# A graph attention and feed-forward kernel: rounded passes on three source tiles instead of one, two of their low parts made by DMA, and earlier loads

## The chip, the cores and the metric

One core of one Trainium2 chip runs the whole program. The metric is the device time in microseconds (us) of one execution, the median of several runs; lower is better.

## The reference

There are N = 1250 nodes with 768 features and 21,250 edges (a list of random pairs in both directions, and one loop per node). Two graph attention layers are followed by a feed-forward block.

```
def gat_layer(x, W, att_src, att_dst, bias, src, dst, heads, out_ch):
    h = (x @ W.T).reshape(n, heads, out_ch)
    e = leaky_relu(a_src[src] + a_dst[dst], 0.2)
    m = segment_max(e, dst);  ex = exp(e - m[dst])
    alpha = ex / (segment_sum(ex, dst)[dst] + 1e-16)
    return segment_sum(alpha[:, :, None] * h[src], dst) + bias

h   = relu(gat_layer(layernorm(x), W1, ..., heads=8, out_ch=128))
x   = x + gat_layer(h, W2, ..., heads=1, out_ch=768)
out = x + ffn(layernorm(x))     # six class tokens take a routed path
```

The change lies almost wholly in the first layer, with its eight heads.

## The kernel before

Attention is dense. A 1250 by 1250 matrix holds the logarithm of the number of edges between each destination and each source (LC, ten tiles of 125 destinations). For a head, the logits of 125 destinations against all 1250 sources are one tile L of 125 by 1250, and L is turned by TensorE so that sources lie on the partitions and the sum over sources is a matmul.

The first layer's loop runs over steps. A step n is one head h = n / 5 (rounded down) and one pair g of destination tiles; there are 5 steps a head and 40 in all. A pair of heads shares one pass of the loop, so k runs from 0 to 9. For step n:

- VectorE makes two logit tiles (L2061, one instruction each), then subtracts the log counts and takes the largest (L2070, one each). It also takes the reciprocals of the sums (L2038, L2040) for 10, 6 or 4 tiles at a time, three times for two heads, and once a head copies one column set (L2052).
- ScalarE takes the exponentials of the two tiles (L897, an ACTIVATE and a read of its accumulator each) and counts `exp_done` up once, after the second.
- TensorE waits for `exp_done` and turns the two tiles with 20 transposes of 125 by 125 into five PSUM banks (L1385), four to a bank, in groups of two source tiles by 250 destinations. After each bank it counts `tb_full`.
- ScalarE copies each bank into the tile PT in SBUF (L915 and, for one bank, L912 and L913), which counts `tb_evac`.
- TensorE sums over the ten source tiles into 125 by 250 of PSUM (L1409), features h1s times PT. A float32 matmul is shown as two instructions. One source tile, number PART = 2, goes in three passes with operands rounded to a shorter format (float32r): high times high, low times high, high times low (L1414 to L1416). ScalarE makes the high parts (L912, L924) and VectorE the low ones by subtraction (L2082, L2087).
- ScalarE copies the sums to hT (L948).

The first head (steps 0 to 4) takes all ten source tiles in float32.

What runs in what order on an engine is fixed by the program. TensorE in its step k does the turning of step k-1, then the sums of step k-2. ScalarE in its step k does this:

```
evac(hh, k)          # the banks of step k-1
exp(hh, k)           # the exponentials of step k
part_higher(hh, k)   # once a head
rows_out_of(hh, k)   # three times for two heads (L936)
sums_out(hh, k)      # the sums of step k-3
```

VectorE in its step k does the logits of step k and then the low part of step k-1. SyncE issues the loads of a head's logits (asb, 1250 KB, a broadcast to all partitions, L488), its features (L483) and small stores of reciprocals; GpSimd does nothing in this stage. Ahead of step k = 6 of the first pair of heads TensorE needs W2 (w2n_sb, 3 MB, L455) for 48 small instructions (L1446). After the last head come the product with W2 (L1481), the second layer and the feed-forward block, which the change leaves alone but for names of semaphores.

## Time and profile before

| | |
|---|---|
| median of 3 runs | 715.89 us (714.38 to 720.05) |
| the profiled execution | 714.73 us |
| its span, first to last instruction | 712.9 us |
| granted TensorE clock, mean | 0.999 of full speed, in the records of every slice 0.9 or more |
| TensorE busy | 700.6 us, 98% |
| VectorE, ScalarE, GpSimd busy | 529.0, 420.3, 106.3 us |

Of the execution's time 1.8 us lie outside the span. Times below are of that one execution, counted from the start of its span. "Busy" is the time in which at least one instruction of the engine is in flight, so a busy engine isn't always one at its peak: a matmul is shown longer than the distance to the next one. What counts for rate is the distance between starts.

### The profile page before, as it was taken

To read this page: it belongs to the slowest core of one execution; us is meant where nothing else is said; L and a number is where in the kernel's file an instruction comes from. 1 tells how busy PE (TensorE), PEld (TensorE's weight loads), DVE (VectorE), ACT (ScalarE), POOL (GpSimd) and SP (SyncE) were. 2 spreads that over 40 slices of the span, in tenths; PEclk is the share of its full clock that TensorE was granted. 3 is DMA by queue.
4 is the path that set the end of the run, shared out by engine and by line. 5 is a ranking of instruction groups with operands and counts; after the bars stand their busy time and mean duration, and the time that the engine had idled before them with its cause. 6 is when DMAs were issued, how large, how long until landed. Compare 5 with 4: busy or idle time off the path is not lost.

```text
span 712.9 us, 13401 instructions
## 1 busy us (share of the span) xinstructions
PE 700.6 (98%) x4670; PEld 657.0 (92%) x4670; DVE 529.0 (74%) x878; ACT 420.3 (59%) x863; POOL 106.3 (15%) x95
## 2 busy tenths in 40 slices
PE   7899999999999999999999999999999999999997
PEld 6699999889799999999999999999999899999997
DVE  5999888698899999999999664445568752737232
ACT  4665584388688889888888754454443333522202
POOL 2558121000000000000000000000123331222202
PEclk9999999999999999999999999999999999999999
DMA  8727656649321212302330443201881735315102
GB/s 284 221 64 202 198 181 174 175 137 315 116 73 37 73 37 73 108 21 88 87 126 0 105 110 71 61 0 36 247 281 55 215 91 189 100 58 176 44 23 67
DMA packets 50226, 84.10 MB, mean 118 GB/s; under 512 B 14633, under 2 KB 35951, under 8 KB 49280
## 3 DMA queue, kind: packets, MB, share of 16 engines
q1 hardware_dynamic: 44492, 65.69, 30.6%
q10 hardware_dynamic: 4500, 13.82, 5.9%
q0 software_dynamic: 1184, 3.92, 1.9%
q8 instruction: 31, 0.51, 0.3%
q14 instruction: 19, 0.16, 0.1%
HBM read 68.09 MB, written 15.33 MB: 117 GB/s over the span
## 4 chain that ended last, share of the span: by engine, by line
PE 87%; DMA 6%; DVE 3%; SPq 1%; ACT 1%; issue 1%; POOL 0%; ACTq 0%; DVEq 0%
PE bank L1409 19%; PE bank L1554 13%; PE bank L1481 12%; PE bank L1281 11%; PE bank L1385 11%; PE bank L1658 4%; PE bank L1630 3%; DMA w1n_sb<-in_W 3%; PE bank L1196 3%; DMA w2n_sb<-in_W 2%; PE bank L1535 2%; PE bank L1684 1%; DVE x2f L2295 1%; PE bank L1198 1%; PE bank L1211 1%; PE bank L1715 1%
## 5 line engine op out<-in xcount | busy, mean ns | idle before, releaser
L1409 PE MATMUL bank<-PT,h1s 125*128 125x250 f32 x730 | 161.0, 374 | 0.0
L1409 PEld LDWEIGHTS bank<-PT,h1s 125*128 125x128 f32 x730 | 135.3, 190 | 14.4
L2061 DVE SCALAR_TENSOR_TENSOR L<-asb,nadh 125x1250 f32<-125x1250 f32 x80 | 117.9, 1514 | 1.9 <-PE bank L1385 0.9
L2070 DVE CUSTOM_DVE_ANT_0 L<-L,LC 125x1250 f32<-125x1250 f32 x80 | 113.4, 1454 | 0.6 <-DMA LC<-log_count_scratch 0.4
L897 ACT ACTIVATE L<-L,nm 125x1250 f32<-125x1250 f32 x80 | 108.3, 1383 | 2.7 <-DVE nm L2070 1.9
L915 ACT COPY PT<-bank 125x500 f32<-125x500 f32 x165 | 87.4, 611 | 36.5 <-PE bank L1385 36.5
L1385 PE MATMUL bank<-ident,L 125*125 125x125 f32 x800 | 94.2, 273 | 0.0
L1385 PEld LDWEIGHTS bank<-ident,L 125*125 125x125 f32 x800 | 91.2, 189 | 0.9 <-issue 0.4
L1867 DVE TENSOR_TENSOR hotr<-iota,r 125x1500 f16<-125x1500 f16 x50 | 46.5, 931 | 8.1 <-PE bank L1198 4.5
L1554 PE MATMUL bank<-h_hi,PT_hi 125*125 125x384 f32 x200 | 41.5, 350 | 0.0
L1554 PE MATMUL bank<-h_lo,PT_hi 125*125 125x384 f32 x200 | 40.4, 342 | 0.0
L726 POOL MEMSET pick<- 128x90 f32 x1 | 0.2, 169 | 268.0 <-ACT hT L948 268.0
L1037 ACT ACTIVATE L<-L,nm 125x1250 f32<-125x1250 f32 x10 | 13.4, 1341 | 42.3 <-DVE nm L2215 42.3
L1554 PE MATMUL bank<-h_hi,PT_lo 125*125 125x384 f32 x200 | 38.1, 336 | 0.0
L1554 PEld LDWEIGHTS bank<-h_hi,PT_hi 125*125 125x125 f32 x200 | 34.0, 185 | 2.5 <-ACT PT_hi L1045 0.7
L2147 DVE COPY as2c<-bank 125x1 f32<-125x1 f32 x10 | 1.6, 158 | 45.6 <-ACT h_hi L1000 45.6
L1554 PEld LDWEIGHTS bank<-h_hi,PT_lo 125*125 125x125 f32 x200 | 35.1, 185 | 0.0
L1554 PEld LDWEIGHTS bank<-h_lo,PT_hi 125*125 125x125 f32 x200 | 34.9, 186 | 0.0
L702 POOL TENSOR_TENSOR x<-x,b_sb 125x768 f32<-125x768 f32 x10 | 19.0, 1901 | 103.6 <-DMA fc2b_sb<-in_fc2b 93.4
L987 ACT ACTIVATE hT<-hT,b_sb x64 | 19.5, 387 | 24.6 <-DVE hT L2122 24.6
L2272 DVE TENSOR_TENSOR x2f<-bank,x2f 125x384 f32<-125x384 f32 x20 | 10.2, 551 | 29.5 <-PE bank L1658 27.9
L1630 PE MATMUL bank<-yT,fc_sb 128*128 128x250 f32 x144 | 31.3, 375 | 0.0
(285 smaller groups left out, 1345.1 us busy)
## 6 DMA issues: line engine op xcount, KB each, us to landing
asb<-src_logit_rows SPq DMA_DIRECT2D x7, 1250.0 KB, 5.8
atom_w<-in_atom_inT SPq DMA_DIRECT2D x5, 1152.0 KB, 12.7
atom_w<-in_atom_outT SPq DMA_DIRECT2D x5, 1152.0 KB, 9.8
log_count_scratch<-LCw SPq DMA_DIRECT2D x10, 546.9 KB
LC<-log_count_scratch SPq DMA_DIRECT2D x10, 546.9 KB
LCt<-log_count_scratch SPq DMA_DIRECT2D x10, 546.9 KB
h_scratch<-h1st ACTq DMA_DIRECT2D x10, 448.0 KB
rdT<-reciprocal_scratch SPq DMA_DIRECT2D x8, 500.0 KB, 4.6
```

What stands on the lines that cost most here:

```text
L897: e = act.activation(L[r][:, :], L[r][:, :], ACT.Exp, bias=nm[q][:, t:t + 1], scale=-1.0, accum_out=den[q][:, t:t + 1])
L915: act.copy(PT[(k - lag) % 2][:, 2 * b:2 * b + 2, :], turned[0:NP, 0:2 * GW].rearrange("p (s n) -> p s n", s=2)).then_inc(tb_evac, 1)
L1281: mm = pe.matmul(bank[b][0:NP, 0:c1 - c0], rows[t % 2][:, k, :], weights[:, k, c0:c1], start=(part == 0 and k == 0), stop=(part == 2 and k ...
L1385: mm = pe.transpose(bank[turned_bank(first, k - lag, b)][0:NP, (2 * s + j) * NP:(2 * s + j + 1) * NP], L[(2 * (k - lag) + j) % 4][:, (2 * ...
L1409: mm = pe.matmul(sums, h1s[q][:, s, :], PT[p][:, s, :], start=(s == 0), stop=(plain and s == NT - 1))
L1481: mm = pe.matmul(bank[2 * p + b][0:NP, 0:w], rows[p][:, k, :], weights[:, k, c0:c0 + w], start=(part == 0 and k == 0), stop=(part == 2 and ...
L1554: mm = pe.matmul(bank[2 + 2 * j + b][0:NP, 0:HALF], rows[:, s, j * NP:(j + 1) * NP], features[:, s, b * HALF:(b + 1) * HALF], start=(term ...
L1630: mm = pe.matmul(bank[6 + m // 2][:, (m % 2) * GW:(m % 2 + 1) * GW], fc1_sb[:, k, m * 128:(m + 1) * 128], yT[:, k, :, :].rearrange("p j n ...
L1658: mm = pe.matmul(bank[down_bank(i, j) + b][0:NP, 0:HALF], rows[:, m, j * NP:(j + 1) * NP], weights[:, m, b * HALF:(b + 1) * HALF], start=( ...
L1867: dve.tensor_tensor(hotr[w][:, :, :, :], iota2[:, 0:GW, :].unsqueeze(1).to_broadcast([CE, TRIP, GW, 2]), r16[:, ds(2 * pair, 2 * TRIP)].re ...
L2061: dve.scalar_tensor_tensor(L[r][:, :], asb[q][0:NP, 1, :], nadh[q][:, t:t + 1], asb[q][0:NP, 0, :], ALU.add, ALU.max).then_inc(stt_done, 1)
L2070: dve.tensor_tensor_reduce(out=L[r][:, :], in0=L[r][:, :], in1=LC[:, t, :], scale=-1.0, scalar=-FLOOR, op0=ALU.add, op1=ALU.min, accum_out ...
```

## The change

Source tiles 0, 1 and 2 of the first layer's sums go in rounded passes instead of tile 2 alone (heads 1 to 7; the first head stays as it was). Tile 0's low part is made by VectorE, as that of tile 2 was. The low parts of tiles 1 and 2 are made by GpSimd's DMA queue: ScalarE writes the turned tile once as it is and once rounded, one of the two with its sign turned, one transfer copies the first into PT_sum, and a second one adds the other to it. The head's first logit loads are split in four, W2 turned (w2n_sb) is loaded during the stage before, W2 itself (w2_sb) in eight pieces during the loop. Some buffers share memory that had their own.

```diff
-PART = 2
+QUARTERS = 4
+PART = 0
...
+                if i == 1:
+                    sp.wait_ge(wattp, 1)
+                else:
+                    load_w2n(i - 2)
...
-            sp.wait_ge(wattp, 1)
-            for k in range(KD):
-                load_w2n(k)
...
                     sp.wait_ge(stt_done, NT * (2 * hh + q) + NT)
-                    load_logits(q, 2 * hh + q + 2)
+                    load_logits(q, 2 * hh + q + 2, 0)
                     (store_even, store_odd_last)[q](hh)
+                    for b in range(1, 3):
+                        sp.wait_ge(stt_done, NT * (2 * hh + q) + (NT + 2 * b))
+                        load_logits(q, 2 * hh + q + 2, b)
                     sp.wait_ge(agg_done, NG * (2 * hh + q) + NG)
                     load_features(q, 2 * hh + q + 2)
-            sp.wait_ge(wattp, 3)
-            sp.dma_start(w2_sb[:, :, 0:D], W2T.rearrange("(k p) n -> p k n", p=128)).then_inc(w2_in, 16)
+                    sp.wait_ge(stt_done, NT * (2 * hh + q) + (NT + 6))
+                    load_logits(q, 2 * hh + q + 2, 3)
+                    sp.wait_ge(wattp, 3)
+                    sp.wait_ge(stt_done, NT * (2 * hh + q) + (NT + 8))
+                    load_w2(2 * hh + q)
...
+            def lower_by_sum(hh, kk):
+                n, p = 2 * NG * hh + kk, kk % 2
+                pool.wait_ge(tb_evac, NG * n + 2)
+                alone(pool)
+                pool.dma_start(PT_sum[p][:, :, :].bitcast(F32), PT[p][:, 1:3, :]).then_inc(raw_moved, 16)
+                pool.wait_ge(raw_moved, 16 * n + (16 - 16 * NG))
+                alone(pool)
+                pool.dma_start(PT_sum[p][:, :, :].bitcast(F32), PT_hi[p][:, 1:3, :].bitcast(F32), accum_op=ALU.add
+                               ).then_inc(lower_moved[p], 16)
...
                     if b == PART // 2 and not (first and k - lag < NG):
-                        act.copy(PT_hi[(k - lag) % 2][:, :], turned[0:NP, 0:GW])
-                        act.copy(PT[(k - lag) % 2][:, PART + 1, :], turned[0:NP, GW:2 * GW]).then_inc(tb_evac, 1)
+                        act.copy(PT_hi[(k - lag) % 2][:, 0:2, :],
+                                 turned[0:NP, 0:2 * GW].rearrange("p (s n) -> p s n", s=2))
+                        act.activation(PT[(k - lag) % 2][:, 1, :], turned[0:NP, GW:2 * GW], ACT.Copy, scale=-1.0
+                                       ).then_inc(tb_evac, 1)
+                    elif b == 1 and not (first and k - lag < NG):
+                        act.copy(PT[(k - lag) % 2][:, 2:4, :],
+                                 turned[0:NP, 0:2 * GW].rearrange("p (s n) -> p s n", s=2))
+                        act.activation(PT_hi[(k - lag) % 2][:, 2, :], turned[0:NP, 0:GW], ACT.Copy, scale=-1.0
+                                       ).then_inc(tb_evac, 1)
...
-                act.copy(h1p[q][:, 0, :], h1s[q][:, PART, :]).then_inc(features_high, 1)
+                act.activation(h1p_neg[q][:, :, :], h1s[q][:, 1:3, :], ACT.Copy, scale=-1.0)
+                act.copy(h1p_hi[q][:, :, :], h1s[q][:, 0:3, :]).then_inc(features_high, 1)
...
-                    pe.matmul(sums, h1p[q][:, 0, :], PT_hi[p][:, :], start=False, stop=False)
-                    pe.matmul(sums, h1p[q][:, 1, :], PT_hi[p][:, :], start=False, stop=False)
-                    mm = pe.matmul(sums, h1p[q][:, 0, :], PT_lo[p][:, :], start=False, stop=True)
+                    for s in range(3):
+                        high = h1p_neg[q][:, 1, :] if s == 2 else h1p_hi[q][:, s, :]
+                        pe.matmul(sums, high, PT_hi[p][:, s, :], start=False, stop=False)
+                        pe.matmul(sums, h1p_lo[q][:, s, :], PT_hi[p][:, s, :], start=False, stop=False)
+                    pe.matmul(sums, h1p_hi[q][:, 0, :], PT_lo[p][:, :], start=False, stop=False)
+                    pe.wait_ge(lower_moved[p], 16 * NG * hh + 16 * ((k - lag) // 2 - (NG // 2 - p)))
+                    pe.matmul(sums, h1p_neg[q][:, 0, :], PT_sum[p][:, 0, :], start=False, stop=False)
+                    mm = pe.matmul(sums, h1p_hi[q][:, 2, :], PT_sum[p][:, 1, :], start=False, stop=True)
...
-                    dve.tensor_tensor(h1p[q][:, 1, :], h1s[q][:, PART, :], h1p[q][:, 0, :].bitcast(F32), ALU.subtract
-                                      ).then_inc(features_lower, 1)
+                    dve.tensor_tensor(h1p_lo[q][:, 0:2, :], h1s[q][:, 0:2, :], h1p_hi[q][:, 0:2, :].bitcast(F32),
+                                      ALU.subtract)
+                    dve.tensor_tensor(h1p_lo[q][:, 2, :], h1p_hi[q][:, 2, :].bitcast(F32), h1s[q][:, 2, :],
+                                      ALU.subtract).then_inc(features_lower, 1)
```

## Rows read from the trace of the kernel before

**Rows 1.** Busy time, the sum over four heads, 209.43 to 336.87 us.

```profile
sum 127.44, PE 127.44 PEld 119.48 DVE 123.90 ACT 110.33 POOL 0.00; mean PE 31.86 PEld 29.87 DVE 30.97 ACT 27.58 POOL 0.00
```

**Rows 2.** Waits from 209 to 395 us: total us, times, longest.

```profile
ACT PT L915 <- PE bank L1385: 25.7, 30, 1.0
DVE dn L2038 <- ACT L L897: 3.0, 6, 0.5
```

**Rows 3.** Timeline of TensorE's weight loads, one step: start, length, instruction.

```profile
311.12 2.27 PEld L1385 LDWEIGHTS bank<-ident,L 125*125 125x125 f32 x20
313.32 3.68 PEld L1409 LDWEIGHTS bank<-PT,h1s 125*128 125x128 f32 x18
317.02 0.19 PEld L1414 LDWEIGHTS bank<-PT_hi,h1p 125*128 125x128 f32 x1
...
317.35 0.19 PEld L1416 LDWEIGHTS bank<-PT_lo,h1p 125*128 125x128 f32 x1
317.47 0.63 PEld L1385 LDWEIGHTS bank<-ident,L 125*125 125x125 f32 x5
```

**Rows 4.** Timeline of ScalarE, the same step.

```profile
311.88 0.58 ACT L915 COPY PT<-bank 125x500 f32<-125x500 f32 x1 [0.71 <-PE bank L1385]
312.35 0.37 ACT L912 CAST PT_hi<-bank 125x250 fp32r<-125x250 f32 x1
312.61 0.39 ACT L913 COPY PT<-bank 125x250 f32<-125x250 f32 x1
312.87 1.57 ACT L915 COPY PT<-bank 125x500 f32<-125x500 f32 x3
314.27 1.39 ACT L897 ACTIVATE L<-L,nm 125x1250 f32<-125x1250 f32 x1
...
315.60 1.38 ACT L897 ACTIVATE L<-L,nm 125x1250 f32<-125x1250 f32 x1
316.83 0.24 ACT L897 ACTIVATION_READ_ACCUMULATOR L<-L,nm 125x1 f32 x1
...
318.22 0.58 ACT L915 COPY PT<-bank 125x500 f32<-125x500 f32 x1 [0.90 <-PE bank L1385]
```

**Rows 5.** Timeline of ScalarE, ahead of that step, where a head begins.

```profile
310.47 0.33 ACT L924 CAST h1p<-h1s 125x128 fp32r<-125x128 f32 x1
310.66 0.25 ACT L936 COPY rrow<-bank 10x125 f32 x1
310.81 0.35 ACT L948 COPY hT<-bank 128x250 f32 x1
```

**Rows 6.** Timeline of VectorE in the same step.

```profile
312.07 0.08 DVE L2070 DVE_READ_ACCUMULATOR2_ANT nm<- 125x1 f32 x1
...
313.45 0.29 DVE L2082 TENSOR_TENSOR h1p<-h1s,h1p 125x128 fp32r<-125x128 f32 x1
313.66 0.41 DVE L2087 TENSOR_TENSOR PT_lo<-bank,PT_hi 125x250 fp32r<-125x250 f32 x1
313.99 2.94 DVE L2061 SCALAR_TENSOR_TENSOR L<-asb,nadh 125x1250 f32<-125x1250 f32 x2
```

**Rows 7.** DMA queues and issues; an issue's size and median us to landing.

```profile
q0 software_dynamic: 1184, 3.92, 1.9%
...
x<-in_x POOLq DMA_DIRECT2D x10, 336.0 KB, 3.6
```

**Rows 8.** Line 698, GpSimd's loads of x: ns of issue, first and last.

```profile
L698 POOL DMA_DIRECT2D x<-in_x x20: 518/552/627, 414.9 to 668.8; - x20
...
DMA to landing us min/median/max: 3.1/3.7/8.7
```

**Rows 9.** Waits of TensorE, 130 to 215 us.

```profile
PE bank L1446 <- DMA w2n_sb<-in_W: 0.8, 1, 0.8
```

**Rows 10.** Timeline behind the last turning, 400 to 404 us.

```profile
402.21 0.42 DVE L2087 TENSOR_TENSOR PT_lo<-bank,PT_hi 125x250 fp32r<-125x250 f32 x1 [5.50 <-ACT PT L913]
...
402.97 0.27 PE L1430 MATMUL bank<-ident,rden 125*4 125x125 f32 x1 [0.20 <-DVE rden L2040]
```

More of the change, by code:

```diff
@@ L293, in gnn_ffn_kernel @@
         L = [sb(f"L{r}", [NP, N], F32, p3) for r in range(4)]
+        once = ExitStack()
+        rdA = [sb(f"rdA{p}", [C, H, NP], F32, once) for p in range(2)]
+        once.close()
         asb[1] = sb("asb1", [128, 2, N], F32, p3)
@@ L427, in gnn_ffn_kernel @@
         w1_hi_done, w1_lo_done, xT_lo_done = sem("w1_hi_done"), sem("w1_lo_done"), sem("xT_lo_done")
+        raw_moved, lower_moved = sem("raw_moved"), [sem(f"lower_moved{p}") for p in range(2)]
         features_high, features_lower, lower_done = sem("features_high"), sem("features_lower"), sem("lower_done")
@@ L548, in load_reciprocals @@
                     sp.wait_ge(scaled, t - 1)
+                if t < 2:
+                    sp.wait_ge(stt_done, NT * H)
                 to = (rdA if t < 2 else rdT)[t % 2]
@@ L721, in after_x2 @@
                     add_bias(n + 1)
+            def lower_by_sum(hh, kk):
[7 more added lines that the diff above has]
+                               ).then_inc(lower_moved[p], 16)
+            for kk in range(NG, 2 * NG):
+                lower_by_sum(0, kk)
+            with pool.Fori(1, H // 2) as hh:
+                for kk in range(2 * NG):
+                    lower_by_sum(hh, kk)
             pool.wait_ge(agg_done, NG * H)
@@ L932, in rows_out_of @@
                 act.wait_ge(rden_turned, m + 1)
-                to = rlast[:, ds(hh if k else hh + -1, 1), 0:NP] if (t0, t1) == (LATE, NT) else None
-                if to is None:
-                    to = rrow[t0:t1, ds(h, 1), 0:NP]
-                act.copy(to.rearrange("t a n -> t (a n)"), bank[4][0:t1 - t0, 0:NP]).then_inc(rden_rows, 1)
+                freed(act, rden_stored, 16 * m)
+                act.copy(rrow[0:t1 - t0, 0:NP], bank[4][0:t1 - t0, 0:NP]).then_inc(rden_rows, 1)
             def sums_out(hh, k, first=False, last=False):
@@ L1407, in aggregate @@
                         pe.wait_ge(head_in[q], TWO * (hh + 1))
-                    if plain or s != PART:
-                        mm = pe.matmul(sums, h1s[q][:, s, :], PT[p][:, s, :], start=(s == 0), stop=(plain and s == NT - 1))
+                    if plain or s > 2:
+                        mm = pe.matmul(sums, h1s[q][:, s, :], PT[p][:, s, :], start=(s == (0 if plain else 3)), stop=(plain and s == NT - 1))
                 if not plain:
@@ L1552, in add_5 @@
                     if j == 0 and b == 0 and s % 2 == 0 and term != "hl":
-                        pe.wait_ge(t5_high if term == "hh" else t5_evac, 5 * i + s // 2 + 1)
+                        if term == "hh":
+                            pe.wait_ge(tb_evac, TURNED_BANKS + 5 * i + s // 2 + 1)
+                        else:
+                            pe.wait_ge(t5_evac, 5 * i + s // 2 + 1)
                     mm = pe.matmul(bank[2 + 2 * j + b][0:NP, 0:HALF], rows[:, s, j * NP:(j + 1) * NP],
```

68 lines of the change are left out of this document (41 added, 27 removed).

## The prediction, as it went on record before the run

> **What bounds the kernel now.** I read three things in this order: the busy times of the stage that the change touches, the waits in it, and then the timelines of one step side by side, to see which loop closes last.
>
> TensorE has no gap at all over four heads: 31.86 us a head, all of it busy, while VectorE is busy for 30.97 and ScalarE for 27.58 [rows 1]. In the same stretch ScalarE waits for TensorE 30 times, 25.7 us in all, and VectorE six times for ScalarE, 3.0 us; no wait of TensorE is among them [rows 2]. So TensorE sets the pace, 6.37 us a step.
>
> One step of TensorE is 2.20 us for 20 transposes (311.12 to 313.32), 3.70 for 18 float32 instructions and 0.45 for the three rounded ones, with the switch to them (317.02 to 317.47): 6.35 [rows 3]. A float32 instruction is 3.70 / 18 = 0.21 us, a source tile 0.42. A rounded pass is 0.12 at most (317.35 to 317.47); I use 0.115, and a tile in three passes is about 0.345.
>
> The reader should see how near the others are. ScalarE is not slow by its sum, but it stands in a loop with TensorE: the turning of step n-1 gives the copies of its banks, then come the two exponentials of step n, and only then may TensorE turn step n, since it waits for `exp_done`. In numbers: the turning's first weight load at 311.12 [rows 3], first copy at 311.88, so 0.76; copies until the first exponential at 314.27, 2.39; the two exponentials until the accumulator is read at 316.83 + 0.24 = 317.07, 2.80 [rows 4]. That is 5.95, and the next turning starts at 317.47 [rows 3]: TensorE comes 0.40 us after ScalarE is ready. The loop would close by itself in 5.95 plus the reaction to one semaphore, which no row shows by itself, since nobody waits there now. I bound it by 0 and 0.10, the distance between two transposes (2.20 / 20 = 0.11), and take 0.03, an estimate. 5.98 against 6.35: the slack is 0.37 us a step.
>
> **The change part by part.**
>
> TensorE. Two tiles go from 0.42 to 0.345, so a step loses 4 x 0.21 - 6 x 0.115 = 0.15 us and needs 6.20. Alone over 35 steps that is 5.3 us.
>
> ScalarE, each step. Before, the five banks are four copies of 500 columns and two of 250. After, they are five of 500 and two of 250: bank 0 is rounded whole and its second half written again with the sign turned, bank 1 is copied whole and its first half rounded again. One copy of 500 more: 0.47 us (311.88 to 312.35; three others take 1.40) [rows 4]. A copy with a scale has no row of that shape; it is the same instruction reading the same bank, so I take the 0.26 of the 250-column pieces (312.35, 312.61, 312.87), and its bounds are 0.26 and 0.47, the 500-column pace. All of it stands between the turning and the exponentials, none in ScalarE's idle time, because that idle time lies behind the exponentials. The loop becomes 5.98 + 0.47 = 6.45 us, longer than TensorE's 6.20 and longer than today's 6.35. This is the core of my forecast: 0.15 is taken off the engine that bounds, 0.47 is put into a loop with a slack of 0.37.
>
> ScalarE, once a head. `part_higher` casts 128 columns in 0.19 (310.47 to 310.66), then 0.15 for the reciprocals' row, then the sums [rows 5]. The change makes 256 and 384 columns of it. By the exponential's pace (1250 columns in 316.83 - 315.60 = 1.23, 0.95 us a thousand [rows 4]) they are 0.31 and 0.43. From the second exponential's start ScalarE's next work may begin after about 1.32, and the next bank is ready after 1.47 + 0.03 + 0.76 = 2.26: 0.94 is free. Needed are 0.31 + 0.43 + 0.15 + 0.26 = 1.15, so 0.21 a head comes on top. Bounds: 0 and 0.74.
>
> A head is then 5 x 6.45 + 0.21 = 32.46 against 31.86: +0.60, and seven heads +4.2 us. The steps' scatter by the unknown reaction (0 to 0.10) is -1.0 to +2.4.
>
> VectorE. Per head the subtraction for the features grows from one of 128 columns (0.21, 313.45 to 313.66) to 256 and 128; 250 columns take 0.33 (313.66 to 313.99) [rows 6], so +0.33. With the 30.97 busy of [rows 1] that is 31.3 and with small gaps 31.5 at most, under 32.46: hidden. If ScalarE's loop were not there, this would be the next bound. PT_lo now reads bank 0 and TensorE's next turning of bank 0 waits for it, but it is made right after the largest of the step ahead is taken, at 313.66, and that step's exponentials end 3.4 us later [rows 4, 6]: hidden, and dear only if VectorE falls 3 us behind. Its largest values are ready at 312.15 and 313.53 for exponentials that start at 314.27 and 315.60 [rows 4, 6], so ScalarE doesn't wait for them, and after the change it asks later still.
>
> GpSimd's two transfers. They run each step one behind the other: 125 rows of 2000 bytes, 250 KB, out of SBUF and into it. The nearest row is the load of x: 336 KB land 3.6 us after issue. The queue moved 3.92 MB in 1.9% of 16 engines' span, 217 us of engine time, so 18 KB a microsecond and engine [rows 7]; 336 KB on 16 engines are 1.16 us and the rest, 2.4 us, is fixed. A 250 KB copy is 2.4 + 0.86 = 3.3. No row shows a transfer that adds. It is at least a copy (3.3), and with its destination read as well its data part at most doubles (4.1). I take 4.1, so with 0.2 for two reactions T = 7.6; in 7.0 to 7.6 without other traffic. One load of x took 8.7 [rows 8], 5 more than its median, beside large loads; that is my upper end for traffic.
> Its deadline: if step n is turned at S, bank 1 is copied at S + 0.76 + 2 x (0.47 + 0.26) = S + 2.2. TensorE turns n+1 from S + 6.45 on for 2.2, then does 14 float32 instructions (2.95) and seven rounded ones (0.8), and asks at S + 12.4. So T may be 10.2, and 7.6 is hidden. GpSimd itself is held for the first transfer and two issues of 0.55 [rows 8], some 4.6 of 6.45 us, and has nothing else queued until the last head's sums are out. The last step is turned with no exponentials behind it, and its transfers have only some 7.9 us; T just fits: 0, at most 1.
>
> The Trainium skill (DMA: Bandwidth & Descriptors, Anatomy of one DMA) fits a GpSimd transfer as 2.0 us plus the bytes at 436 KB a microsecond. By it the pair would take an estimated 5.1 us and the deadline would be met with more room; the forecast is the same by either, and the rows' larger value is used above.
>
> Loads. W2 is 0.8 us late for TensorE now [rows 9]; loaded a stage earlier it isn't: -0.8. The six loads stand in SyncE's queue behind the wait for the first stage's small product and between stores and loads of log counts; TensorE has no wait on a DMA from 130 us on but this one [rows 9], so I take 0 for the added traffic, bounds 0 and +2. The queue's logits in four pieces and eight W2 pieces add some ten issues a head and waits on VectorE's logits; each is for a tile that is due a head later. Cost 0; if a store of reciprocals behind them came late, ScalarE would wait for its row buffer, which has become single, but it has three steps or more. W2 itself was there early before: 0.
>
> End of the stage. The last two sums have no exponentials to wait for, so TensorE's 0.15 counts there: -0.3. VectorE's last PT_lo waits for bank 0 instead of bank 1 and with it the 0.20 that TensorE waits for the last reciprocals [rows 10] goes: -0.2.
>
> Sum: +4.2 - 0.8 - 0.3 - 0.2 = +2.9. On the profiled execution's 714.7 that is 717.6 us. Its time lies 1.2 under the median of the three runs, within their spread of 5.7.
>
> **The rivals.**
>
> A. The loop through ScalarE doesn't close as I say (its instructions overlap more, or the scaled copies are cheaper), and TensorE or VectorE bounds. For it: the page's sum leaves ScalarE idle 4.3 us a head [rows 1]. Against it: that idle time lies wholly in front of the first copy of a step, where it waits for TensorE [rows 2, 4]. Price: with TensorE alone -5.3 - 1.0 = 708.4; with VectorE at 31.5 a head -0.36 x 7 - 1.0, 711.2.
>
> B, the slow side. The two transfers miss the deadline in every step. The mechanism: 125 rows don't divide by 16. If a transfer is spread over the largest number of engines up to 16 that divides its rows, that is 5, the data part of a copy is 250 / 5 / 18 = 2.8 and that of an adding one up to 5.6. The pair takes 5.2 + 8.0 + 0.2 = 13.4. It decides from T = 10.2 on: then the loop runs over two steps through PT's two buffers, T + 0.25 + 0.76 + 1.46 long, and a step is (T + 2.5) / 2 = 7.9 us, +1.6 x 35 = 770. If only the adding one is spread so, T = 11.5, a step is 7.0, +22, 738. For it: every long transfer of this program that goes to 125 rows is cut into 112 and 13 (ROWS in the code), the new ones aren't, and no row shows one uncut. Against it: the median over all twenty loads of x, half of them of 13 rows, is 3.7 [rows 8], and that of the large ones 3.6 [rows 7], so the fixed part is most of such a transfer.
> The Trainium skill (DMA: Bandwidth & Descriptors, Why a DMA increments its semaphore by 16 and not by 1) states this rule of the largest divisor, and an exception in which GpSimd's plain copies take all 16 engines with rows rounded up. No row here tells which holds for an adding transfer.
>
> C. T is short enough alone, but not beside the head's features (625 KB in short pieces) or a quarter of the logits: then one or two steps a head run over. By the 8.7 of [rows 8] T is up to 12.6, 2.4 over: seven times 1.2 to 2.4, 726 to 735.
>
> **How the numbers follow.** My forecast has 0.55, A 0.15 (a third of it at TensorE's bound), B 0.18, C 0.12. The likeliest case alone runs from 714 to 721. A measurement of this kernel can tell about 1% from no change, 7 us. The range leaves out the lower end of A and the upper part of B: 709 to 738. Faster by over 1% (under 708.7) is the end of A alone, 0.06. Slower by over 1% (over 723) is B, C and the tail of mine where several upper bounds meet: 0.18 + 0.12 + 0.03 = 0.33. Within 1%: 0.61.
>
> **What would show it.** In the changed kernel's profile a plain step should be 6.45 us between turnings, TensorE should have a gap ahead of most turnings (0.25 us, released by the exponential of L897), ScalarE's wait for bank 0 should shrink to what the first four transposes take, and be gone at a head's beginning. GpSimd's second transfers should land before the last two matmuls ask; a gap inside the sums, released by a DMA to PT_sum, is B or C. The 0.8 us before L1446 should be gone. The forecast is wrong if turnings follow each other in 6.2 to 6.3 us without a gap (A), or if gaps stand inside the sums (B, C).

## The result, and the profile after it

The changed kernel takes 737.38 us (median of 4 runs, 734.57 to 739.14) against 715.68 (714.38 to 720.05) for the kernel before: ratio 1.0307, 95% interval 1.0281 to 1.0334. It is slower by 21.7 us where the forecast was +2.9; 737.4 lies 0.6 us inside the upper end of the range of 709 to 738, an end that stands for another case than the one that came. The profiled execution took 737.6 us, its span is 735.8 us against 712.9, so 22.9 us are to be found. Its mean granted TensorE clock is 0.994, that of before 0.999.

The page of the changed kernel, first the busy times, then its GpSimd DMA queue and the two transfers (KB each, median us from issue to landing):

```profile
PE 708.1 (96%) x4740; PEld 661.9 (90%) x4740; DVE 532.1 (72%) x885; ACT 440.7 (60%) x905; POOL 162.1 (22%) x165
...
q0 software_dynamic: 8464, 21.43, 14.8%
...
PT_sum<-PT POOLq DMA_DIRECT2D x35, 244.1 KB, 3.6
PT_sum<-PT_hi POOLq DMA_DIRECT2D x35, 244.1 KB, 4.2
```

TensorE's share has fallen from 98% to 96%, though its matmuls of a step were to take 0.15 us less. The waits of TensorE over the whole span (us in total, times, longest) say where that is:

```profile
PE bank L1471 <- DMA PT_sum<-PT_hi: 13.1, 8, 3.0
PE bank L1436 <- ACT L L942: 2.8, 15, 0.3
```

L1471 is the first of the two matmuls that read PT_sum: TensorE stands inside the sums, released by the adding transfer. L1436 is the turning, released by the exponentials. Both are waits that [rows 2] does not have. For nearly the same stretch as [rows 2], here 209 to 410 us, the same view has also the waits of the other engines:

```profile
POOL PT_sum L759 <- DMA PT_sum<-PT: 113.9, 29, 6.1
...
ACT PT_hi L957 <- PE bank L1436: 23.5, 23, 2.9
```

Before, ScalarE waited 30 times for bank 0, once for each turning. Now it is 23 times for 29 turnings, up to 2.9 us where TensorE itself came late, and the six turnings without a wait are the ones behind ScalarE's extra work of a head's beginning, as the prediction said.

**An undisturbed step.** The weight loads of TensorE, same view as [rows 3]: a turning begins every 6.62 us, not every 6.35 as in those rows (317.47 less 311.12), and ahead of each there is a gap. For a weight load the view calls what ends the gap "issue"; for the matmul behind it, it names the exponentials of L942, as above:

```profile
244.77 2.26 PEld L1436 LDWEIGHTS bank<-ident,L 125*125 125x125 f32 x20 [0.36 <-issue]
...
251.38 2.26 PEld L1436 LDWEIGHTS bank<-ident,L 125*125 125x125 f32 x20 [0.25 <-issue]
...
308.82 2.26 PEld L1436 LDWEIGHTS bank<-ident,L 125*125 125x125 f32 x20 [0.35 <-issue]
...
315.43 2.26 PEld L1436 LDWEIGHTS bank<-ident,L 125*125 125x125 f32 x20 [0.37 <-issue]
```

ScalarE in the step whose turning begins at 308.82, same view as [rows 4]:

```profile
309.56 0.58 ACT L957 CAST PT_hi<-bank 125x500 fp32r<-125x500 f32 x1 [0.69 <-PE bank L1436]
310.03 0.38 ACT L959 ACTIVATE PT<-bank 125x250 f32<-125x250 f32 x1
310.30 0.58 ACT L962 COPY PT<-bank 125x500 f32<-125x500 f32 x1
310.75 0.41 ACT L964 ACTIVATE PT_hi<-bank 125x250 fp32r<-125x250 f32 x1
311.02 1.57 ACT L967 COPY PT<-bank 125x500 f32<-125x500 f32 x3
312.42 1.40 ACT L942 ACTIVATE L<-L,nm 125x1250 f32<-125x1250 f32 x1
...
313.75 1.38 ACT L942 ACTIVATE L<-L,nm 125x1250 f32<-125x1250 f32 x1
314.98 0.25 ACT L942 ACTIVATION_READ_ACCUMULATOR L<-L,nm 125x1 f32 x1
```

Turning to first copy 0.74 (308.82 to 309.56), copies 2.86 (to 312.42), exponentials 2.81 (to 314.98 + 0.25 = 315.23). The next turning begins at 315.43: 0.20 us after ScalarE is done. This is the loop of the prediction, closed, and the copies with a scale cost what was said, 0.27 for 250 columns (310.03 to 310.30 and 310.75 to 311.02).

**A disturbed step.** GpSimd's timeline has an undisturbed pair of transfers and one beside loads. The idle time in brackets ahead of L759 runs from the end of the first issue to the landing of the copy:

```profile
219.97 0.55 POOL L756 DMA_DIRECT2D PT_sum<-PT  x1 [2.29 <-ACT PT L967]
226.57 0.84 POOL L759 DMA_DIRECT2D PT_sum<-PT_hi  x1 [6.06 <-DMA PT_sum<-PT]
...
247.69 0.55 POOL L756 DMA_DIRECT2D PT_sum<-PT  x1 [2.45 <-ACT PT L967]
251.02 0.84 POOL L759 DMA_DIRECT2D PT_sum<-PT_hi  x1 [2.77 <-DMA PT_sum<-PT]
```

Alone, the copy took 3.3 us from the start of its issue to the start of the next (247.69 to 251.02), that is 2.8 behind the end of its issue of 0.55; the one at 219.97 took 6.6 and 6.1. The median to landing that the views give (3.6) counts from the end of the issue, as its lowest of 2.8 and highest of 6.9 show. SyncE's queue and the windows (us from, to, length; busy of each engine; granted clock; DMA share; GB/s) show what was in the air with it:

```profile
218.34 1.49 SPq L503 DMA_DIRECT2D asb<-src_logit_rows  x2
223.68 0.95 SPq L497 DMA_DIRECT2D h1s<-h_scratch  x2
224.89 0.35 SPq L503 DMA_DIRECT2D asb<-src_logit_rows  x1
```

```profile
219.00:221.00 2.00, 2.00 (x13) 1.85 (x12) 2.00 (x6) 2.00 (x6) 0.55 (x1) 1.00 0.95 170
...
247.00:251.00 4.00, 4.00 (x25) 3.68 (x25) 4.00 (x6) 4.00 (x8) 0.55 (x1) 1.00 0.42 95
...
264.00:266.00 2.00, 0.32 (x3) 0.12 (x1) 1.41 (x3) 0.76 (x3) 0.00 (x0) 1.00 1.05 271
...
267.00:268.00 1.00, 1.00 (x6) 1.00 (x6) 0.80 (x2) 0.34 (x1) 0.43 (x1) 0.50 0.01 3
...
270.00:271.00 1.00, 1.00 (x9) 0.94 (x9) 0.40 (x1) 0.84 (x2) 0.48 (x1) 1.00 0.95 140
```

The copy started on full engines (share 0.95, two quarters of the logits), and the adding transfer then ran into the features and a third quarter. The pair took 11.3 us (219.97 to 231.26) where 7.6 were forecast and 10.2 were to be free. The waits of TensorE that follow, in its timeline:

```profile
231.26 0.39 PE L1471 MATMUL bank<-PT_sum,h1p_neg 125*128 125x250 f32 x1 [1.38 <-DMA PT_sum<-PT_hi]
266.20 0.38 PE L1471 MATMUL bank<-PT_sum,h1p_neg 125*128 125x250 f32 x1 [1.88 <-DMA PT_sum<-PT_hi]
...
425.40 0.38 PE L1471 MATMUL bank<-PT_sum,h1p_neg 125*128 125x250 f32 x1 [1.87 <-DMA PT_sum<-PT_hi]
...
432.62 0.38 PE L1471 MATMUL bank<-PT_sum,h1p_neg 125*128 125x250 f32 x1 [2.95 <-DMA PT_sum<-PT_hi]
432.96 4.52 PE L1537 MATMUL bank<-w_hi,h1Tt_hi 128*125 128x384 f32 x16
```

About one step a head has such a wait, 34 to 36 us apart (203.47, 231.26, 266.20, 301.93, 336.04, 370.56; between the first two it is 28), of 1.1 to 1.9 us, and the last two steps of the stage have 1.87 and 2.95. These eight are the 13.1 us.

**The clock.** Behind the wait of 1.88 us (264 to 266 us, TensorE busy for 0.32 of 2.00), the windows show a granted clock of 0.50, that is 1.2 instead of 2.4 GHz, with TensorE busy all the time; at 270 it is 1.00 again. Its weight loads show what that costs:

```profile
266.47 3.90 PEld L1436 LDWEIGHTS bank<-ident,L 125*125 125x125 f32 x20
...
274.39 2.27 PEld L1436 LDWEIGHTS bank<-ident,L 125*125 125x125 f32 x20
```

The turning takes 3.90 us instead of 2.26 and the step 7.92 instead of 6.62: 1.3 us. Behind the wait of 2.95 the first 16 matmuls of the product with W2 take 4.36 to the next group (432.96 to 437.32); without transfers (the first experiment) it is 3.37, another 1.0 us. But a wait doesn't always bring this. Behind 1.38 the next step is 6.62 long, and behind 1.87, nearly as long as the wait of 1.88, the granted clock stays at 1.00 (425 to 432 us) and the 14 float32 matmuls take 2.77 us as elsewhere.

### The profile page after: what moved, and what is told of

It reads as the page before. It is cut to its first block, busy times and chain, and to the rows that moved or that the text cites. A ratio compares the mean times of both kernels' runs of the same rounds, so it can differ in the third digit from the quotient of the medians.

```text
span 735.8 us, 13937 instructions
## 1 busy us (share of the span) xinstructions
PE 708.1 (96%) x4740; PEld 661.9 (90%) x4740; DVE 532.1 (72%) x885; ACT 440.7 (60%) x905; POOL 162.1 (22%) x165
## 4 chain that ended last, share of the span: by engine, by line
PE 72%; DMA 15%; ACT 6%; DVE 3%; issue 3%; ACTq 0%; POOL 0%; SPq 0%; POOLq 0%; DVEq 0%
PE bank L1613 13%; PE bank L1537 12%; PE bank L1332 11%; PE bank L1460 8%; PE bank L1436 7%; DMA PT_sum<-PT 6%; DMA PT_sum<-PT_hi 5%; PE bank L1717 4%; DMA w1n_sb<-in_W 3%; PE bank L1689 3%; PE bank L1247 3%; ACT L L942 2%; PE bank L1591 1%; PE bank L1743 1%; DVE x2f L2356 1%
## 5 line engine op out<-in xcount | busy, mean ns | idle before, releaser
L1460 PE MATMUL bank<-PT,h1s 125*128 125x250 f32 x590 | 131.4, 374 | 0.0
L1460 PEld LDWEIGHTS bank<-PT,h1s 125*128 125x128 f32 x590 | 108.9, 190 | 11.2
L942 ACT ACTIVATE L<-L,nm 125x1250 f32<-125x1250 f32 x80 | 108.6, 1389 | 2.8 <-DVE nm L2129 1.9
L1436 PE MATMUL bank<-ident,L 125*125 125x125 f32 x800 | 98.2, 279 | 3.8 <-ACT L L942 2.8
L1436 PEld LDWEIGHTS bank<-ident,L 125*125 125x125 f32 x800 | 92.4, 191 | 9.5 <-issue 8.6
L967 ACT COPY PT<-bank 125x500 f32<-125x500 f32 x130 | 67.3, 626 | 2.1 <-PE bank L1436 2.1
L759 POOL DMA_DIRECT2D PT_sum<-PT_hi x35 | 29.6, 845 | 142.8 <-DMA PT_sum<-PT 136.7
L756 POOL DMA_DIRECT2D PT_sum<-PT x35 | 20.9, 596 | 91.0 <-ACT PT L967 91.0
L957 ACT CAST PT_hi<-bank 125x500 fp32r<-125x500 f32 x35 | 20.1, 574 | 31.4 <-PE bank L1436 31.4
```

Source lines behind the costliest of these rows:

```text
L759: pool.dma_start(PT_sum[p][:, :, :].bitcast(F32), PT_hi[p][:, 1:3, :].bitcast(F32), accum_op=ALU.add).then_inc(lower_moved[p], 16)
L942: e = act.activation(L[r][:, :], L[r][:, :], ACT.Exp, bias=nm[q][:, t:t + 1], scale=-1.0, accum_out=den[q][:, t:t + 1])
L967: act.copy(PT[(k - lag) % 2][:, 2 * b:2 * b + 2, :], turned[0:NP, 0:2 * GW].rearrange("p (s n) -> p s n", s=2)).then_inc(tb_evac, 1)
L1436: mm = pe.transpose(bank[turned_bank(first, k - lag, b)][0:NP, (2 * s + j) * NP:(2 * s + j + 1) * NP], L[(2 * (k - lag) + j) % 4][:, (2 * ...
L1460: mm = pe.matmul(sums, h1s[q][:, s, :], PT[p][:, s, :], start=(s == (0 if plain else 3)), stop=(plain and s == NT - 1))
```

## The experiments

Each was timed against the kernel before on the same chip, whose medians were 714.5 to 715.3 us in these comparisons. Theory: two costs that add, the loop through ScalarE (copies with a scale, nothing else) and transfers that miss their deadline only beside loads. Rivals: the transfers are too slow by themselves (the prediction's B), or the time is lost elsewhere, in the early loads or in GpSimd's use of the queue.

**1. No transfers.** ScalarE does all its work, TensorE all its passes.

```diff
-            for kk in range(NG, 2 * NG):
-                lower_by_sum(0, kk)
-            with pool.Fori(1, H // 2) as hh:
-                for kk in range(2 * NG):
-                    lower_by_sum(hh, kk)
...
-                    pe.wait_ge(lower_moved[p], 16 * NG * hh + 16 * ((k - lag) // 2 - (NG // 2 - p)))
-                    pe.matmul(sums, h1p_neg[q][:, 0, :], PT_sum[p][:, 0, :], start=False, stop=False)
-                    mm = pe.matmul(sums, h1p_hi[q][:, 2, :], PT_sum[p][:, 1, :], start=False, stop=True)
+                    pe.matmul(sums, h1p_neg[q][:, 0, :], PT_hi[p][:, 0, :], start=False, stop=False)
+                    mm = pe.matmul(sums, h1p_hi[q][:, 2, :], PT_hi[p][:, 1, :], start=False, stop=True)
```

> The changed kernel without GpSimd's two transfers and without TensorE's wait for them; its last two matmuls of a step read PT_hi in place of PT_sum, so the low parts of source tiles 1 and 2 are left out of the result. ScalarE's scaled copies stay. Theory 1 (the loop through ScalarE costs a fixed 0.25 us a step, the late transfers the rest): a step stays at 6.62 us in all steps, 723 to 726 us, so 9 over before. Theory 2 (the transfers cost everything, the copies are hidden): 716 or less.

721.61 us (721.21 to 723.27), ratio 1.0091 (1.0064 to 1.0119), span 721.5; the median is 1.4 us under the range expected, with the steps as expected. The transfers cost 14.3 us of span; 8.6 of the 22.9 are there without them. The steps are as long as the undisturbed ones of the changed kernel (weight loads of TensorE):

```profile
223.61 2.26 PEld L1430 LDWEIGHTS bank<-ident,L 125*125 125x125 f32 x20 [0.36 <-issue]
230.22 2.26 PEld L1430 LDWEIGHTS bank<-ident,L 125*125 125x125 f32 x20 [0.37 <-issue]
```

**2. No copies with a scale.** The transfers stay; the second one reads what is there.

```diff
-                        act.activation(PT[(k - lag) % 2][:, 1, :], turned[0:NP, GW:2 * GW], ACT.Copy, scale=-1.0
-                                       ).then_inc(tb_evac, 1)
...
-                        act.activation(PT_hi[(k - lag) % 2][:, 2, :], turned[0:NP, 0:GW], ACT.Copy, scale=-1.0
-                                       ).then_inc(tb_evac, 1)
...
-                pool.dma_start(PT_sum[p][:, :, :].bitcast(F32), PT_hi[p][:, 1:3, :].bitcast(F32), accum_op=ALU.add
+                pool.dma_start(PT_sum[p][:, :, :].bitcast(F32), PT_hi[p][:, 0:2, :].bitcast(F32), accum_op=ALU.add
```

> The changed kernel without ScalarE's two scaled copies a step: the transfers move what lies in PT and PT_hi, of the same size, and TensorE takes PT_hi's slot 1 for tile 2, so tiles 1 and 2 are not summed rightly. Transfers and waits stay. Theory 1: ScalarE's loop falls to 6.1 us and TensorE or VectorE paces the plain steps at 6.2 to 6.4; the transfers are late as often and by more, since steps are shorter: 725 to 730. Theory 2: as the changed kernel, 737, since the copies were hidden.

730.87 us (727.33 to 733.66), ratio 1.0220 (1.0172 to 1.0269), 0.9 us above what was expected. A plain step is 6.20, but TensorE waits more for the transfers, since a shorter step is also a shorter deadline (waits of TensorE):

```profile
PE bank L1467 <- DMA PT_sum<-PT_hi: 14.2, 7, 4.9
```

**3. Neither.** Both edits together.

> Both left out: no transfers, no scaled copies; the low parts of tiles 1 and 2 are left out and tile 2's high part is that of slot 1. It shows what the rounded passes are worth by themselves. By TensorE's 0.15 us a step and the earlier load: 708.5 to 710; if VectorE's 31.3 to 31.5 us a head paces it: 711 to 713. Both theories expect less than before.

708.92 us (708.65 to 709.88), ratio 0.9918 (0.9890 to 0.9946). This is the change with everything that it adds to ScalarE's steps and to GpSimd's queue taken out, and it comes out at rival A's price (708.4). Weight loads of TensorE, then a window over nearly 20 steps:

```profile
214.96 2.27 PEld L1426 LDWEIGHTS bank<-ident,L 125*125 125x125 f32 x20
221.16 2.27 PEld L1426 LDWEIGHTS bank<-ident,L 125*125 125x125 f32 x20
```

```profile
208.67:332.00 123.33, 123.33 (x859) 117.17 (x858) 122.41 (x162) 110.07 (x212) 0.00 (x0) 1.00 0.29 76
```

TensorE has no gap and a plain step is 6.20, the figure of the prediction; some are 6.29 to 6.32. VectorE is busy 122.41 of 123.33 us: it is 0.05 us a step from being the bound.

The four corners, in us to the kernel before (by ratio): neither -5.9, copies alone +6.5, transfers alone +15.7, both +22.0. Copies are worth 12.4 without the transfers and 6.3 with them: by the medians the two costs overlap by half of the smaller one. The reason that I give, that a longer step leaves the transfers more time, is argued and not measured by itself, and the 6.3 is rough: the runs of the second experiment spread over 6 us.

**4. GpSimd adds instead of its queue.** One addition takes the place of the two transfers; the result is the whole.

```diff
-                pool.dma_start(PT_sum[p][:, :, :].bitcast(F32), PT[p][:, 1:3, :]).then_inc(raw_moved, 16)
...
+                pool.tensor_tensor(PT_sum[p][:, :, :], PT[p][:, 1:3, :], PT_hi[p][:, 1:3, :].bitcast(F32), ALU.add
+                                   ).then_inc(raw_moved, 1)
...
+                    pe.wait_ge(raw_moved, n + (1 - NG))
```

> The changed kernel with one addition on GpSimd a step in place of the two transfers (same operands, same result). Theory 1: the addition of 500 columns takes some 1.3 us, far under its deadline of 10, and the kernel is as without transfers, 723 to 727; up to 2 us more if VectorE's instructions with two operands in SBUF are held up by it. Theory 2: 716 or less.

742.05 us (741.68 to 742.29), ratio 1.0378 (1.0350 to 1.0407): missed by far, worse than the transfers. The timeline shows VectorE as the bound, where I had allowed for 2 us. VectorE's operation for the largest value, alone and beside GpSimd's addition:

```profile
304.85 1.45 DVE L2128 CUSTOM_DVE_ANT_0 L<-L,LC 125x1250 f32<-125x1250 f32 x1
305.90 1.51 POOL L758 TENSOR_TENSOR PT_sum<-PT,PT_hi 125x500 fp32r<-125x500 f32 x1 [5.50 <-ACT PT_hi L963]
...
306.23 2.50 DVE L2128 CUSTOM_DVE_ANT_0 L<-L,LC 125x1250 f32<-125x1250 f32 x1
...
308.77 1.34 ACT L941 ACTIVATE L<-L,nm 125x1250 f32<-125x1250 f32 x1 [0.27 <-DVE nm L2128]
```

```profile
296.00:396.00 100.00, 89.79 (x599) 82.83 (x600) 99.34 (x111) 84.42 (x172) 25.00 (x14) 1.00 0.24 64
```

The addition takes 1.8 us (median), and TensorE never waits for it. But VectorE takes 2.50 instead of 1.45, and it had only 0.37 us a step to spare (in the first experiment, with the same steps, it is busy for 93.75 us of 15 steps, 99.35 us). Now it is busy for 99.34 of 100 us (the window), TensorE for 89.79, and the second exponential waits for VectorE. Steps are 7.0 to 7.8 us (turnings at 303.41, 310.41, 317.42, 325.17). The Trainium skill (SBUF — State Buffer, Who interferes with whom) says that a VectorE instruction with two inputs in SBUF contends with a GpSimd instruction that reads SBUF; L2128 reads L and LC, and the trace agrees, at 1.05 us for this pair.

**5. No transfers, and ScalarE in another order.** As the first, but ScalarE copies banks 0 and 1, makes the exponentials, and copies the rest; TensorE waits bank by bank.

```diff
-                evac(hh, k, **at_end)
-                if not ahead:
+                if ahead:
+                    evac(hh, k, **at_end)
+                else:
+                    evac(hh, k, banks=range(2), **at_end)
                     exp(hh, k, **at_end)
+                    evac(hh, k, banks=range(2, 5), **at_end)
...
-                elif b == 0 and not (first and k == lag):
-                    pe.wait_ge(tb_evac, NG * n)
+                elif not (first and k == lag):
+                    pe.wait_ge(tb_evac, NG * n + (b + 1 - NG))
```

> As e1 (no transfers, scaled copies kept, low parts of tiles 1 and 2 left out), but ScalarE copies banks 0 and 1 of step n-1, takes the exponentials of step n, then copies banks 2 to 4, and TensorE waits for each bank by itself. Same work on every engine; only the loop from one turning to the next is shorter, by 1.4 us. Theory 1 (it is the loop, not ScalarE's sum of work): TensorE paces it, a step is 6.2 us, 708.5 to 711, as e3. Rival (the copies cost by their work, wherever they stand): 720 to 722, as e1.

710.96 us (709.12 to 716.35), ratio 0.9955 (0.9930 to 0.9981). ScalarE does every instruction of the first experiment, and 10.7 us are gone (9.7 by the two ratios): it is the place of the copies in the loop that costs, not ScalarE's work. Turnings of TensorE:

```profile
217.18 2.27 PEld L1433 LDWEIGHTS bank<-ident,L 125*125 125x125 f32 x20
223.38 2.27 PEld L1433 LDWEIGHTS bank<-ident,L 125*125 125x125 f32 x20
```

**6. The changed kernel with its loads spread.** One quarter of the logits or half of the features every one or two tiles, instead of in clusters.

```diff
                     load_logits(q, 2 * hh + q + 2, 0)
+                    sp.wait_ge(stt_done, NT * (2 * hh + q) + (NT + 2))
+                    load_logits(q, 2 * hh + q + 2, 1)
                     (store_even, store_odd_last)[q](hh)
...
+                    load_features(q, 2 * hh + q + 2, 0, 5)
+                    sp.wait_ge(stt_done, NT * (2 * hh + q) + (NT + 8))
+                    load_features(q, 2 * hh + q + 2, 5, 10)
+                    sp.wait_ge(stt_done, NT * (2 * hh + q) + (NT + 9))
                     load_logits(q, 2 * hh + q + 2, 3)
```

> The changed kernel, all of it right, with the head's loads spread: logits quarters at tiles 0, 2, 4 and 9 of the next head, W2's piece with the third, the features in two halves at tiles 6 and 8, and the store of reciprocals behind the second quarter. Same bytes. Theory 1 (the transfers are late only beside bunches of loads): the waits of 1.3 to 3 us once a head shrink below 0.5 and the kernel comes to 723 to 728. Rival (the two transfers are too long by themselves): 735 to 739.

733.90 us (732.50 to 737.29), ratio 1.0280 (1.0232 to 1.0329): under the rival's range and far over the first theory's, so missed by both; the interval overlaps that of the changed kernel (1.0281 to 1.0334). Waits of TensorE, and the landing of the copy (L760 there):

```profile
PE bank L1475 <- DMA PT_sum<-PT_hi: 9.9, 9, 2.9
...
PT_sum<-PT POOLq DMA_DIRECT2D x35, 244.1 KB, 4.2
```

The waits fall only from 13.1 to 9.9 us, and the median copy goes from 3.6 to 4.2: the collisions are spread with the loads, not avoided. The spread was also less than meant: in the trace a quarter of the logits, W2's piece and the features still begin within 6 us (252.02, 253.54, 257.29), and the step that was late at 266.20 in the changed kernel is late again, at 264.49. What loads that stand farther apart would do, no run shows.

**7. One transfer instead of two.** ScalarE writes what the first transfer brought straight to PT_sum, rounded.

```diff
-                        act.activation(PT[(k - lag) % 2][:, 1, :], turned[0:NP, GW:2 * GW], ACT.Copy, scale=-1.0
+                        act.activation(PT_sum[(k - lag) % 2][:, 0, :], turned[0:NP, GW:2 * GW], ACT.Copy, scale=-1.0
                                        ).then_inc(tb_evac, 1)
...
-                        act.copy(PT[(k - lag) % 2][:, 2:4, :],
-                                 turned[0:NP, 0:2 * GW].rearrange("p (s n) -> p s n", s=2))
+                        act.copy(PT_sum[(k - lag) % 2][:, 1, :], turned[0:NP, 0:GW])
+                        act.copy(PT[(k - lag) % 2][:, 3, :], turned[0:NP, GW:2 * GW])
...
-                pool.dma_start(PT_sum[p][:, :, :].bitcast(F32), PT[p][:, 1:3, :]).then_inc(raw_moved, 16)
-                pool.wait_ge(raw_moved, 16 * n + (16 - 16 * NG))
```

> The changed kernel with the first of the two transfers taken out: ScalarE writes PT_sum itself (rounded, so that the low parts of tiles 1 and 2 come out as next to nothing) and only the adding transfer stays, which lands 4.2 us after issue. Loads are where they were. Theory 1: with 6 us to spare it meets the deadline beside the loads, and what is left is ScalarE's loop, 0.05 us a step longer than in e1: 722 to 725. Rival (any DMA traffic of GpSimd in the loop slows the others): 728 or more.

722.90 us (722.03 to 725.11), ratio 1.0124 (1.0085 to 1.0162), no wait of TensorE on PT_sum at all. The adding transfer by itself:

```profile
DMA to landing us min/median/max: 3.8/3.9/6.0
```

With its issue of 0.84 that is 4.7 us, and 6.8 at worst beside the same loads: it hides wholly. So it is the chain of two that fails. The lowest and the median are far from the 8.0 us that rival B gives an adding transfer without other traffic.

**8. Order of the fifth with the loads of the sixth, both transfers.** The diffs are those above; the result is the whole.

> The changed kernel, all of it right, with both remedies, the order of e5 and the loads of e6. Theory 1: steps of 6.2 us, but the deadline comes 0.8 us earlier than with steps of 6.62, so some transfers are late again: 712 to 722. If the loads' spread is enough: 709 to 712, faster than before. If the transfers are too long by themselves: over 728.

732.93 us (730.84 to 736.21), ratio 1.0268 (1.0215 to 1.0320): missed. It lies in the range that was kept for "too long by themselves", but only nine of the 35 pairs let TensorE wait, so that isn't the cause. The loop is gone (the plain step is 6.20), but nothing is won, since the shorter step asks earlier for PT_sum (waits of TensorE, 9.9 us in the sixth), and the clock falls at three of the waits:

```profile
PE bank L1478 <- DMA PT_sum<-PT_hi: 14.1, 9, 3.1
```

**9. Two rounded tiles instead of three.** As the eighth, with tile 2 left plain: only tile 1's low part is transferred, 122 KB a time, and one of ScalarE's copies with a scale is gone.

```diff
-                pool.dma_start(PT_sum[p][:, :, :].bitcast(F32), PT[p][:, 1:3, :]).then_inc(raw_moved, 16)
+                pool.dma_start(PT_sum[p][:, 0, :].bitcast(F32), PT[p][:, 1, :]).then_inc(raw_moved, 16)
...
-                    for s in range(3):
-                        high = h1p_neg[q][:, 1, :] if s == 2 else h1p_hi[q][:, s, :]
+                    for s in range(2):
+                        high = h1p_hi[q][:, s, :]
```

> All right in its result: order of e5, loads of e6, but only tiles 0 and 1 in rounded passes; tile 1's low part by two transfers of 122 KB instead of 244. TensorE needs 6.27 us a step. The pair should take 6.3 to 6.6 us without other traffic, against a deadline of some 9.7. Theory 1: 711 to 715, faster than before by up to 0.5%, with two or three late steps of up to 1.5 us left. If half the bytes change little beside the loads: 716 to 724.

715.91 us (713.36 to 717.76, 12 runs), ratio 1.0002 (0.9985 to 1.0019), just above what was expected. Half the bytes land 2.3 and 3.5 us behind their issues (medians); one wait of 2.4 us is left:

```profile
PE bank L1476 <- DMA PT_sum<-PT_hi: 2.4, 1, 2.4
```

TensorE's step is 6.27 (turnings at 216.01, 222.28, 228.54), 0.1 less than before, which over 33 steps gives 2.5 us. It comes out even because the stage's end takes them back: the one wait of 2.4, and behind it the granted clock falls to 0.50, and the next 16 matmuls take 4.43 us (411.93 to 416.36) instead of 3.08 before.

**10. Order of the fifth, one transfer as in the seventh.** The changed kernel with the two diffs given there, and its loads as they were.

> Order of e5 with e7's single adding transfer (PT_sum written rounded by ScalarE, so the low parts of tiles 1 and 2 come out as next to nothing), loads as in the changed kernel. It shows what the change would be worth if one transfer could do it. Theory 1: the transfer lands within its time beside the loads as well, 709 to 712. Rival (a transfer in each step slows loads or engines by itself): 716 or more.

709.96 us (708.82 to 712.17), ratio 0.9929 (0.9903 to 0.9955), 1.0 us above the third. With the loop opened and one transfer in place of two, both costs are gone, and of the 22 us no more than about 1 remains.

**11. The kernel before with W2 turned loaded early.** One part of the change alone; the result is the whole.

```diff
+                if i == 1:
+                    sp.wait_ge(wattp, 1)
+                else:
+                    load_w2n(i - 2)
...
-            sp.wait_ge(wattp, 1)
-            for k in range(KD):
-                load_w2n(k)
```

> The kernel before with one part of the change: W2 for the small product is loaded in six pieces during the first stage. Theory 1: TensorE's wait of 0.8 us goes and nothing is late for it, 0.1% faster at best, which the measurement can hardly tell: 713.5 to 716. Rival (3 MB more beside the stores and loads of log counts delay the first stage): 717 to 719, with new waits of TensorE before 130 us.

713.29 us (712.66 to 714.43, 12 runs) against 714.99 (23 runs), ratio 0.9971 (0.9958 to 0.9984), 0.2 us under what was expected: 0.3% faster than the kernel before and 3.3% faster than the changed one, the only version here with the whole arithmetic that beats both. TensorE goes over without a wait (timeline):

```profile
176.78 1.64 PE L1410 MATMUL bank<-PT,h1s 125*128 125x250 f32 x7
178.35 2.77 PE L1447 MATMUL bank<-w2n_sb,att 128*2 128x256 f32 x48
```

## Why the prediction was right in its range and wrong in its mechanism

**The number, and luck.** That 737.4 lies inside 709 to 738 is luck. The upper end was set by one form of rival B, an adding transfer spread over five engines (738), and that didn't happen. My likeliest case ran from 714 to 721. What happened is C, late transfers once a head, whose own sum ended at 735, on top of a loop that costs nearly twice what I said (+7.9 us and not +4.2), and with losses at the stage's end and in clock that no sum held in full. Its own sign of being wrong, gaps inside the sums, was there.

**The account.** Of 22.9 us of span, 8.6 are there without transfers. By stages, in us, from the starts of turnings and of the product with W2 in the three traces:

| | before | without transfers (1) | changed |
|---|---|---|---|
| start to the turning of step 6 | 190.0 | 190.7 | 189.6 |
| 33 steps, to the turning of step 39 | 210.3 | 218.2 | 227.5 |
| to the product with W2 | 11.2 | 10.6 | 15.9 |
| to the end of the span | 301.4 | 302.0 | 302.8 |

Without transfers the loop takes 7.9 more (30 of the 33 steps are 6.63 on the average instead of 6.37), the stage's end 0.6 less; 1.3 more ahead of the loop and behind the stage have no cause that I found. With the transfers come 9.3 in the loop (six late steps, 1.0 to 1.8 us each, and 1.3 for the slower clock), 5.3 at the stage's end (the waits of 1.87 and 2.95) and 0.9 behind it, where the clock costs 1.0; the stages ahead of step 6 take 1.2 less. A late step costs a little less than its wait, since the wait takes the place of the 0.2 us that TensorE would have waited for ScalarE.

**TensorE, 6.20 a step.** Right: experiment 3.

**ScalarE's copies, +0.47, and the loop as the new bound.** Right in place and price, and shown from both sides: without the copies (3), or with them behind the exponentials (5), the plain step is 6.20. Mis-sized is the term "plus the reaction to one semaphore": I took 0.03, bounded by 0.10 from the distance between two transposes, and it is 0.20 to 0.22. The row was the wrong one. Two transposes in a row say how fast TensorE issues, not how long it takes from an end on ScalarE to a start on TensorE. 0.18 in 35 steps are 6.3 us; the steps that the loop paces in the trace are 30. Once a head it was 0.09 instead of 0.21.

**VectorE hidden.** Right; "this would be the next bound" is right too: at 6.20 a step it is 99% busy (3).

**T = 7.6 and the deadline of 10.2.** Near, and both a little too kind. The transfers themselves are shorter than I said, 2.8 and 3.8 behind their issues instead of 3.3 and 4.1, but I had read the landing times as if they held the issues; with 0.55 and 0.84 the pair is 8.0. It also starts later: in the turning that begins at 244.77 the first issue (247.69) stands 2.9 us behind the turning's start and not 2.2, since GpSimd takes 0.6 us from the end of the copy it waits for (311.16) to its issue (311.74), and TensorE asks at 12.55 (257.32): 9.6 are free. The margin alone is 1.6 us, not 2.6. The step that failed is "and 7.6 is hidden" as the case to expect, with 0.12 for rival C. C is what happened, with one late step a head at 1 to 2 us. I had its evidence in hand, a load of x that took 8.7 instead of 3.7 [rows 8], and the logits' and features' loads stand in every head. Two transfers one behind the other have more chances to meet a load, and even 2.6 us of margin are less than the 5 by which that load was late. It should have been the likeliest case. C's sum, 726 to 735, is short by the loop's 6 us and by what follows here.

**End of the stage, "T just fits: 0, at most 1".** Wrong: 4.8 us of waits and 1.0 of clock. The last pairs went out at 413.49 and 421.53, beside the loads of reciprocals (500 KB each, issued at 411.68 and 422.13), and their copies took 7.4 and 6.8 us with their issues. The last one was also late in starting, since GpSimd was held by the pair ahead until 421.5. I had counted the deadline without asking which loads the stage's end starts. The other two terms of this stage, -0.3 and -0.2, are right: in the first experiment, without transfers, the same place has no wait and is 0.6 us shorter than before.

**The clock.** No rival had it: behind a wait on PT_sum TensorE can lose another 1.0 to 1.3 in clock, as it did behind two of the eight. That may be part of why runs differ: the one at 734.57 had a mean granted clock of 1.000, the other three, 737.16 to 739.14, had 0.994 or 0.995.

**Rival B, transfers over five engines.** Wrong: it needed 5.2 and 8.0 us; alone they took 2.8 and 3.8. The Trainium skill's exception, by which some direct copies of GpSimd's take all 16 engines (DMA: Bandwidth & Descriptors, Why a DMA increments its semaphore by 16 and not by 1), fits the 2.8, and the adding transfer's 3.8 fits it too; how many engines took part was not measured.

**W2 turned early, -0.8.** The wait is gone in every kernel that has it, and the kernel before gains 1.7 us (11; 1.1 to 3.0 by the interval). Where that is more than 0.8, its cause is open. In the changed kernel the gain is smaller than I said: TensorE's turning behind the small product begins at 182.37 instead of 182.85, with 0.3 us of waiting for ScalarE (L987) in the old wait's place, and in the first and third experiments nothing of the 0.8 is seen at that point (183.53 and 182.77). **W2 in pieces, other loads, buffers:** 0 was right; the third experiment has all of them and comes out at A's price.

**What stays open.** No run left out the loads beside the pair, so that they are what delays it is read from the traces (late pairs stand beside them, pairs without them take 8.0) and not tested by itself. Why a transfer beside a load of 300 to 600 KB takes twice as long although the engines are not full all the time (at 221 to 223 us the DMA share is 0.41 and the copy of 219.97 is still in the air) was not taken apart. What decides whether the clock falls behind a wait is open too.

## What to carry to other kernels

Before taking 0.15 us off the engine that bounds, close the next loop with its waits: here it had 0.40 less one reaction of 0.20 to spare, and the change put 0.47 into it; a reorder of that engine's work (5) gave all of it back. A chain of two transfers has to be priced beside the largest loads of its stage and against the deadline of the faster kernel, not of today's, because every microsecond taken from a step is taken from the deadline too (2, 8). And count each wait of the bounding engine with the clock that it may lose after it.

## What the runs showed of the hardware that I had not expected

- From the end of a ScalarE instruction to the start of the TensorE instruction that waits for it: 0.20 to 0.22 us (315.23 to 315.43, 308.60 to 308.82).
- A GpSimd transfer that adds 244 KB (125 rows of 2000 bytes, SBUF to SBUF) takes 0.84 us to issue and lands 3.8 to 3.9 us behind the end of it; the plain one takes 0.55 and 2.8. Beside loads the plain one took up to 6.9 in the changed kernel and 8.2 in the eighth experiment.
- GpSimd's issue starts 0.6 us after the end of the ScalarE copy for which it waits.
- A VectorE operation on 1250 columns with two operands in SBUF goes from 1.45 to 2.50 us beside a GpSimd addition of 500 columns.
- The length of TensorE's wait alone doesn't tell whether the granted clock falls to 0.50. It fell behind waits of 1.88 and 2.95 us (changed kernel), 1.85 and 2.80 (eighth experiment) and 2.40 (ninth); it stayed at 1.00 behind 1.87 (changed kernel), 2.86 (sixth) and 2.38 (eighth).
